# The stand-alone recurrence of a two-layer decoder: order of its work on five engines

## What is computed

```python
def _L0_attn_ref(x, Wk, Wv, Wr, Wo, spatial_decay, spatial_first, mix_k, mix_v, mix_r):
    # q_shift_1d: channels 0..31 come from the token before, 32..63 from the token after, the rest stay
    xx = q_shift_1d(x)
    xk = x * mix_k + xx * (1.0 - mix_k)          # the same for v and r
    k = jnp.einsum('btc,oc->bto', xk, Wk)        # the same for v and r
    sr = jax.nn.sigmoid(r)
    # scan over t with w = decay / T, u = first / T, both states starting at 0:
    #   eku = exp(u + k_t);  out = (a + eku * v_t) / (b + eku);  ek = exp(k_t)
    #   a = a * exp(w) + ek * v_t;  b = b * exp(w) + ek
    return jnp.einsum('btc,oc->bto', sr * wkv_out, Wo)
x = _layernorm(x + _L0_attn_ref(x, ...), axis=-1)
x = _layernorm(x + _L0_xattn_ref(x, ctx_1024, ...), axis=-1)   # and four more sub-layers
```

## Time and profile before

| | |
|---|---|
| median of 3 runs | 2066.99 us (2064.95 to 2070.55) |
| the profiled execution | 2069.05 us, of which 2067.3 us are the span from its first to its last instruction |
| PE busy | 1879.9 us, 91% of the span |
| DVE busy | 1430.0 us, 69% |
| ACT busy | 1191.4 us, 58% |
| POOL busy | 565.3 us, 27% |
| mean granted TensorE clock | 0.961 |
| stage 0 | from the start to 59.65 us, 2.9% of the span |

### The profile page before, as it was taken

How to read it: one execution, slowest core, us unless ns; L and a number is a source line. 1 busy time by engine, 2 the same in 40 slices (tenths; PEclk the granted TensorE clock), 3 DMA queues, 4 the chain that set the end, 5 groups by cost and what they waited for, 6 DMA issues and landing times.

```text
span 2067.3 us, 47928 instructions
## 1 busy us (share of the span) xinstructions
PE 1879.9 (91%) x16935; PEld 1490.1 (72%) x16935; DVE 1430.0 (69%) x3597; ACT 1191.4 (58%) x3980; POOL 565.3 (27%) x894
## 2 busy tenths in 40 slices
PE   3899999999999999999599999788887887699998
PEld 1788888888888888887377777566665554567776
DVE  5578788888887887776465766478786798354443
ACT  1577676676767767766244544277775666133333
POOL 1132222322223221111221221144544576021110
PEclk8899999999999999999799999899999999599999
DMA  7100000000000000000200000100000000000000
GB/s 223 28 2 2 2 2 2 2 2 2 2 2 2 2 2 2 2 2 2 71 1 1 1 1 1 36 2 2 2 2 12 22 12 2 0 0 11 11 4 17
DMA packets 30226, 25.68 MB, mean 12 GB/s; under 512 B 5276, under 2 KB 26788, under 8 KB 29992
## 3 DMA queue, kind: packets, MB, share of 16 engines
q1 hardware_dynamic: 29992, 22.62, 3.8%
HBM read 20.52 MB, written 2.10 MB: 11 GB/s over the span
## 4 chain that ended last, share of the span: by engine, by line
issue 62%; POOL 16%; POOLq 10%; PE 10%; DVE 1%; DMA 0%; DVEq 0%; ACT 0%
POOL X L1817 3%; POOL work L931 3%; PE bank L1938 2%; PE bank L1925 2%; PE bank L1927 2%; POOL work L1608 2%; POOLq L934 2%; POOLq L911 1%; POOL H L935 1%; POOL work L1033 1%; POOL X L1618 1%; PE bank L1905 1%; POOL work L912 1%; POOLq L1607 1%; POOLq L1816 1%
## 5 line engine op out<-in xcount | busy, mean ns | idle before, releaser
L682 ACT ACTIVATE work<-bank,work 128x128 f32<-128x128 f32 x1024 | 363.1, 402 | 208.2 <-DVE work L761 208.2
L523 PE MATMUL bank<-work,wbig 128*128 128x128 f32 x2048 | 262.4, 277 | 0.5 <-ACT work L745 0.5
L523 PEld LDWEIGHTS bank<-work,wbig 128*128 128x128 f32 x2048 | 246.1, 193 | 1.2 <-ACT work L745 0.8
L682 ACT ACTIVATION_READ_ACCUMULATOR work<-bank,work 128x1 f32 x1024 | 246.5, 241 | 0.0
L768 DVE TENSOR_TENSOR work<-work 128x512 f32<-128x512 f32 x256 | 179.1, 700 | 19.8 <-issue 0.9
L761 DVE TENSOR_REDUCE work<-bank 128x4 f32<-128x512 f32 x256 | 159.0, 684 | 33.6 <-PE bank L562 33.6
L697 ACT ACTIVATE work<-bank 128x512 f32<-128x512 f32 x256 | 168.8, 660 | 23.2 <-PE bank L536 23.2
L536 PE MATMUL bank<-ident,work 128*128 128x128 f32 x1024 | 158.1, 277 | 11.8 <-DVE work L768 11.8
L536 PEld LDWEIGHTS bank<-ident,work 128*128 128x128 f32 x1024 | 114.5, 141 | 58.7 <-issue 31.3
L2098 DVE TENSOR_TENSOR work<-wff,bank 128x320 f32<-128x320 f32 (+1 forms) x128 | 62.5, 489 | 127.7 <-ACT wff L2013 127.2
L1167 ACT ACTIVATE work<-bank,col_b 128x512 f32<-128x512 f32 x128 | 87.2, 687 | 106.5 <-PE bank L1095 106.3
(11 more groups left out here) (314 smaller groups left out, 4045.7 us busy)
## 6 DMA issues: line engine op xcount, KB each, us to landing
wbig<-in_moe_w SPq DMA_DIRECT2D x2, 1536.0 KB, 9.2
work<-in_mask_l SPq DMA_DIRECT2D x8, 256.0 KB, 2.9
out<-X SPq DMA_DIRECT2D x8, 256.0 KB, 2.3
H<-in_moe_w SPq DMA_DIRECT2D x3, 512.0 KB, 5.6
wff<-in_moe_w SPq DMA_DIRECT2D x1, 1024.0 KB
X<-in_x SPq DMA_DIRECT2D x1, 512.0 KB, 4.2
wbig<-in_sa_wq SPq DMA_DIRECT2D x1, 512.0 KB, 3.8
wbig<-in_sa_wk SPq DMA_DIRECT2D x1, 512.0 KB, 4.6
```

What stands on the lines that cost most here:

```text
L523: last = nc.tensor.matmul(o[:, j * T:(j + 1) * T], w[:, t * 128:(t + 1) * 128], src, start=True, stop=True)
L682: last = nc.scalar.activation(at_probs[:, g, h, :], bank[g][:, h * T:(h + 1) * T], ACT.Exp, bias=at_nmax[:, g, h:h + 1], accum_out=at_den[ ...
```

## The change

Four things are reordered, and no arithmetic changes.

1. POOL clears the tiles of stage 0 and `b2_sb` first and marks `setup_done`, then clears `keymask` and marks again; the small constants, the tiles of the pairs and `upper` follow without a mark. ACT and VectorE wait for the first mark. VectorE marks, then waits for all four marks before it fills `keymask`. PE waits for all four marks too, but only between the turns and the products.
2. PE turns both groups' tokens first, group 0 into bank 0 and group 1 into bank 7. The output product of group 0 goes to bank 7 and that of group 1 to bank 0.
3. PE forms key and receptance first (mark `rk.kr`), then value (mark `rk.v`). ACT waits for `kr` alone, and VectorE begins with the scan of b, which needs no value, before it waits for `v`.
4. VectorE's `state` is split into `state` and `gate` (reciprocal and z). Its order becomes state(0), gate(0), state(1), residual(0), gate(1), normal(0), residual(1), normal(1). `rk_mv`, `rk_rstd` and `rk_res` get a tile for each group (the second `rk_res` lies on `rk_er[0]`).

The pairs of stage 1 now count on `rk.kr` and `rk.v` instead of semaphores of their own.

```diff
--- before.py
+++ after.py
@@ -129,7 +129,8 @@
 
             xT = sem("rk_xT")
             shift_sb = sem("rk_shift_sb")
-            kvr = sem("rk_kvr")
+            kr = sem("rk_kr")
+            v = sem("rk_v")
             exps = sem("rk_exps")
             gated = sem("rk_gated")
             y = sem("rk_y")
@@ -140,8 +141,6 @@
         class rp:
 
             mixed = sem("rp_mixed")
-            kr = sem("rp_kr")
-            v = sem("rp_v")
             v_sb = sem("rp_v_sb")
             num = sem("rp_num")
             den = sem("rp_den")
@@ -333,37 +332,44 @@
         rk_num = r.take(NB, T)
         rk_den = r.take(NB, T)
         rk_z = [r.take(NB, T) for _ in range(2)]
-        rk_res = r.take(NB, D)
+        rk_res = [r.take(NB, D), rk_er[0]]
         rk_stats = r.take(NB, 6)
-        rk_mv = r.take(NB, 2)
+        rk_mv = [r.take(NB, 2) for _ in range(2)]
         rk_var = r.take(NB)
-        rk_rstd = r.take(NB)
+        rk_rstd = [r.take(NB) for _ in range(2)]
         AHEAD = 2
 
         def flat(ap):
             return ap.rearrange("p b t -> p (b t)")
 
         def rwkv_pe(pe):
+            def turn(g):
+                for b in range(NB):
+                    last = nc.tensor.transpose(bank[7 * g][:, b * T:(b + 1) * T], X[:, NB * g + b, :], ident[:])
+                last.then_inc(rk.xT, 1)
+
+            def product(g, k):
+                o = bank[1 + 3 * g + k]
+                nc.tensor.matmul(o[:], rk_scaled[:, k, 0, :], flat(rk_xT[g]), start=True, stop=False)
+                return nc.tensor.matmul(o[:], rk_scaled[:, k, 1, :], flat(rk_xx[g]), start=False, stop=True)
+
             def front(g):
-                need(pe, rk.shift_sb, g)
-                for b in range(NB):
-                    last = nc.tensor.transpose(bank[0][:, b * T:(b + 1) * T], X[:, NB * g + b, :], ident[:])
-                last.then_inc(rk.xT, 1)
                 pe.wait_ge(rk.shift_sb, g + 1)
-                for k in range(3):
-                    o = bank[1 + 3 * g + k]
-                    nc.tensor.matmul(o[:], rk_scaled[:, k, 0, :], flat(rk_xT[g]), start=True, stop=False)
-                    last = nc.tensor.matmul(o[:], rk_scaled[:, k, 1, :], flat(rk_xx[g]), start=False, stop=True)
-                last.then_inc(rk.kvr, 1)
+                product(g, 0)
+                product(g, 2).then_inc(rk.kr, 1)
+                product(g, 1).then_inc(rk.v, 1)
 
             def back(g):
                 pe.wait_ge(rk.gated, g + 1)
-                need(pe, rk.res_sum, g)
+                pe.wait_ge(rk.shift_sb, 2 - g)
                 for b in range(NB):
-                    last = nc.tensor.matmul(bank[7][:, b * T:(b + 1) * T], rk_z[g][:, b, :], w_rwkv[:, 3, :],
+                    last = nc.tensor.matmul(bank[7 - 7 * g][:, b * T:(b + 1) * T], rk_z[g][:, b, :], w_rwkv[:, 3, :],
                                             start=True, stop=True)
                 last.then_inc(rk.y, 1)
 
+            for g in range(AHEAD):
+                turn(g)
+            pe.wait_ge(setup_done, 4)
             for g in range(AHEAD):
                 front(g)
             for g in range(AHEAD):
@@ -372,25 +378,27 @@
         def rwkv_act(act):
             for g in range(AHEAD):
                 act.wait_ge(rk.xT, g + 1)
-                src = bank[0][:, :].rearrange("p (b t) -> p b t", b=NB)
-                nc.scalar.activation(flat(rk_xT[g]), bank[0][:, :], ACT.Copy)
+                src = bank[7 * g][:, :].rearrange("p (b t) -> p b t", b=NB)
+                nc.scalar.activation(flat(rk_xT[g]), bank[7 * g][:, :], ACT.Copy)
                 nc.scalar.activation(rk_xx[g][0:32, :, 1:T], src[0:32, :, 0:T - 1], ACT.Copy)
                 nc.scalar.activation(rk_xx[g][32:64, :, 0:T - 1], src[32:64, :, 1:T], ACT.Copy)
                 nc.scalar.activation(rk_xx[g][64:128], src[64:128], ACT.Copy).then_inc(rk.shift_sb, 1)
             for g in range(AHEAD):
-                act.wait_ge(rk.kvr, g + 1)
+                act.wait_ge(rk.kr, g + 1)
                 k_ = bank[1 + 3 * g][:, :].rearrange("p (b t) -> p b t", b=NB)
                 nc.scalar.activation(rk_ek[g][:, :, 1:T], k_[:, :, 0:T - 1], ACT.Exp)
                 nc.scalar.activation(flat(rk_eku[g]), bank[1 + 3 * g][:, :], ACT.Exp, bias=rk_u[:, 0:1])
                 nc.scalar.activation(flat(rk_er[g]), bank[3 + 3 * g][:, :], ACT.Exp, scale=-1.0).then_inc(rk.exps, 1)
 
         def rwkv_dve(dve):
+            tt = nc.vector.tensor_tensor
+
             def state(g):
                 dve.wait_ge(rk.exps, g + 1)
+                nc.vector.tensor_tensor_scan(flat(rk_b), flat(rk_ew), flat(rk_ek[g]), 0.0, ALU.mult, ALU.add)
+                dve.wait_ge(rk.v, g + 1)
                 v = bank[2 + 3 * g][:, :].rearrange("p (b t) -> p b t", b=NB)
-                tt = nc.vector.tensor_tensor
                 tt(rk_ekv[:, :, 1:T], rk_ek[g][:, :, 1:T], v[:, :, 0:T - 1], ALU.mult)
-                nc.vector.tensor_tensor_scan(flat(rk_b), flat(rk_ew), flat(rk_ek[g]), 0.0, ALU.mult, ALU.add)
                 tt(flat(rk_num), flat(rk_eku[g]), bank[2 + 3 * g][:, :], ALU.mult)
                 dve.drain()
                 nc.vector.tensor_tensor_scan(flat(rk_a), flat(rk_ew), flat(rk_ekv), 0.0, ALU.mult, ALU.add)
@@ -399,32 +407,37 @@
                 tt(flat(rk_num), flat(rk_num), flat(rk_a), ALU.add)
                 nc.vector.scalar_tensor_tensor(flat(rk_den), flat(rk_er[g]), 1.0, flat(rk_b), ALU.add, ALU.mult)
                 dve.drain()
+
+            def gate(g):
                 nc.vector.reciprocal(flat(rk_den), flat(rk_den))
                 dve.drain()
                 tt(flat(rk_z[g]), flat(rk_num), flat(rk_den), ALU.mult).then_inc(rk.gated, 1)
+                dve.drain()
 
             def residual(g):
                 dve.wait_ge(rk.y, g + 1)
-                nc.vector.tensor_tensor(flat(rk_res), bank[7][:, :], X4[:, g, :], ALU.add).then_inc(rk.res_sum, 1)
+                nc.vector.tensor_tensor(flat(rk_res[g]), bank[7 - 7 * g][:, :], X4[:, g, :], ALU.add).then_inc(rk.res_sum, 1)
                 dve.drain()
                 for b in range(NB):
-                    nc.vector.bn_stats(rk_stats[:, b, :], rk_res[:, b, :])
+                    nc.vector.bn_stats(rk_stats[:, b, :], rk_res[g][:, b, :])
                 dve.drain()
                 for b in range(NB):
-                    last = nc.vector.bn_aggr(rk_mv[:, b, :], rk_stats[:, b, :])
+                    last = nc.vector.bn_aggr(rk_mv[g][:, b, :], rk_stats[:, b, :])
                 last.then_inc(rk.stats, 1)
+                dve.drain()
 
             def normal(g):
                 dve.wait_ge(rk.rstd, g + 1)
                 for b in range(NB):
-                    nc.vector.tensor_scalar(X[:, NB * g + b, :], rk_res[:, b, :], rk_mv[:, b, 0:1], rk_rstd[:, b:b + 1],
-                                            ALU.subtract, ALU.mult)
+                    nc.vector.tensor_scalar(X[:, NB * g + b, :], rk_res[g][:, b, :], rk_mv[g][:, b, 0:1],
+                                            rk_rstd[g][:, b:b + 1], ALU.subtract, ALU.mult)
                 dve.drain()
 
             state(0)
+            gate(0)
+            state(1)
             residual(0)
-            dve.drain()
-            state(1)
+            gate(1)
             normal(0)
             residual(1)
             normal(1)
@@ -432,9 +445,9 @@
         def rwkv_pool(pool):
             for g in range(AHEAD):
                 pool.wait_ge(rk.stats, g + 1)
-                nc.gpsimd.tensor_tensor(rk_var, rk_mv[:, :, 1], lneps[:, 0:NB], ALU.add)
+                nc.gpsimd.tensor_tensor(rk_var, rk_mv[g][:, :, 1], lneps[:, 0:NB], ALU.add)
                 pool.drain()
-                nc.gpsimd.tensor_tensor(rk_rstd, rk_var, half[:, 0:NB], ALU.pow).then_inc(rk.rstd, 1)
+                nc.gpsimd.tensor_tensor(rk_rstd[g], rk_var, half[:, 0:NB], ALU.pow).then_inc(rk.rstd, 1)
                 pool.drain()
 
 
@@ -595,11 +608,11 @@
             def pair_kr(i, o):
                 pe.wait_ge(rp.mixed, 2 * i + 1)
                 pair_product(o, 0, 0)
-                pair_product(o, TWO * T, 2).then_inc(rp.kr, 1)
+                pair_product(o, TWO * T, 2).then_inc(rk.kr, 1)
 
             def pair_v(i, o):
                 pe.wait_ge(rp.mixed, 2 * i + 2)
-                pair_product(o, 0, 1).then_inc(rp.v, 1)
+                pair_product(o, 0, 1).then_inc(rk.v, 1)
 
             def pair_y(i, o):
                 pe.wait_ge(rk.gated, AHEAD + i + 1)
@@ -699,7 +712,7 @@
 
             def pair_shift(i, src):
                 act.wait_ge(rk.xT, AHEAD + i + 1)
-                need(act, rp.v, i)
+                act.wait_ge(rk.v, AHEAD + i)
                 src = src[:, 0:TWO * T].rearrange("p (b t) -> p b t", b=TWO)
                 nc.scalar.activation(rp_xT, src, ACT.Copy)
                 nc.scalar.activation(rp_xx[0:32, :, 1:T], src[0:32, :, 0:T - 1], ACT.Copy)
@@ -707,7 +720,7 @@
```

(25 more changed lines are left out.)

## The result

The changed kernel takes 2056.39 us in the median (2055.06 to 2057.80, 6 runs), the kernel before 2067.89 on the same chips (2064.95 to 2070.56, 6 runs). The ratio is 0.9943, with a 95% interval of 0.9931 to 0.9956: 11.5 us less, as a change of 9 to 14 us. The profiled execution took 2057.20 with a span of 2055.3.

What follows compares the result with a forecast made beforehand. The first stage was taken as bound by a chain from engine to engine; 8.45 us (2.76 from a, 1.25 from b, 4.44 from c) plus 2.11 gave 10.56, so 2066.99 - 10.6 = 2056.4 us, range 2051 to 2062.

Steps and rivals of the forecast that it cites:

- nine links: First stage's chain, from ACT free for the shift (9.72 us) to the next stage's first turn (49.09).
- (c): Key and receptance first: PE's first product to ACT's first exponential takes 6.34 us; 4.44 us of the gain.
- (a): POOL's new clearing order: ACT waits only for the mix columns and is free at 9.72; 2.76 us gained.
- (b): PE turns both groups' tokens before ACT is free: 1.25 us gained; early turns buy no clock.
- (d): VectorE's state(0) starts at 20.13 instead of 28.58, 1.76 us behind the exponentials; value and keymask cost nothing.
- (e): VectorE's interleaving of the groups: the idle 2.17 us before y(0) are covered; z to z shrinks by 2.11 us.
- rival 1: Stage 0's end: engines wait for the last column instead; with landings 3 us later 2058.6 us; chance 0.09.
- Rival 2: Later stage openings: shifted low clock stretches give half back, 5 us over three openings, 2061.4, or reverse, 2052; chance 0.10.

Runs made afterwards that it cites:

- the five undoings: Changed kernel with one part undone each: POOL's order, turns ahead of the wait, group 1's early turns, ACT not waiting for value, interleaving; medians 2061.47, 2059.09, 2060.31, 2059.77, 2059.38.
- The swap: Changed kernel with the two waits at the head of ACT's stream swapped, POOL's mark first, then the mix columns; median 2058.93 us, ratio 0.9954.
- the kernel with the shorter chain: Changed kernel without the reciprocal of group 1, so it doesn't compute the reference; median 2056.69 us, ratio 0.9943.

## Why the prediction was right

**The chain.** The forecast read the first stage as a chain of links and moved each with its duration from the rows. Eight of nine links came out within 0.1 us, and the five undoings started the next stage within 0.2 us of what their links say, but for the 0.7 us of link (c) in the run without POOL's order. The next stage started 11.60 us earlier where 10.56 were summed.

**The term that was mis-sized is (a).** It took ACT's preamble as 2.37 us from its start to its end, table load included, behind the mix columns at 7.25. In the kernel before both waits were over when the load ran, so the earlier trace rows couldn't show which of them the load stood behind. In the changed kernel it needs POOL's mark alone, and 1.28 of the 2.37 us are hidden in the wait for the columns: 8.59 instead of 9.72, with the columns in at 7.40 rather than 7.25. That it was hidden is luck: nothing in the forecast asked in which order the two waits are written. The swap puts them back (+1.33). The sign I gave for being wrong in (a) was a table load *later* than 7.3; it came earlier. The first exponential at 17.30 lies just outside the 17.4 to 19.1 that I gave for (c), for this reason only: link (c) itself was 6.31 for 6.34.

**(b), (c).** Right: the turns were hidden, and the clock rose where group 0's did before. In the eleven kernels in which ACT waited for key and receptance alone (the changed kernel and all experiments but the two that made it wait for more), first product to first exponential took between 5.58 and 6.65 us, inside the bounds of -1.0 and +0.7. The rise is read from the products, 0.86 and then 0.43 us apart; the profile's granted clock reads 1.00 over both, and only from the later low stretch of the earlier trace rows (0.51) is it seen that 0.86 apart goes with the lower level. That early turns buy no clock isn't shown: with identical code up to the first exponential the link took 5.93 to 6.62, and the two extremes of position, turns over 7.2 us ahead of the products (5.58, without POOL's order) and 1.5 us ahead (6.11, turns behind the wait), differ by less than that.

**(d), (e).** Right, link by link; value was never waited for, keymask's 4.97 us ended at 14.2, and y(0) was covered.

**The loads (rival 1).** The margin was read rightly as thin, but the cap was put in the wrong place. The forecast set the column's landing, 48.3, against PE's first turn and capped the gain at 11.3 us; the gain at that turn was 11.60, and it came at 48.05. PE's turn doesn't wait for rows and columns, ACT's copy 0.6 us behind it does. That copy had 1.1 us in hand over the last column in the profiled execution, and would have had 0.2 with the latest landing seen; the kernel with the shorter chain ran into it, and got 0.1 of 3.8 us. The changed kernel is within about a microsecond of what this list of waits allows.

**The median.** That 2056.39 meets 2056.4 is partly luck. I subtracted 10.6 from 2066.99; with three more runs the kernel before stands at 2067.89, and the gain was 11.5. The excess is, within the runs' spread, the mis-sized term's 1.1. Rival 2 (the clock elsewhere) exists, with about 2.7 us beside one added low stretch, more than the 1.65 that I gave one, and fell on neither side in the medians.

## What to carry to other kernels

Where no engine is busy for long, read the stage as a chain: ask of each link what its start waits for, and look for work that stands in an engine's order ahead of what the chain needs (here group 1's turns and shift, value's product, a residual that waits for PE); moving it is worth its full length. Then find what is late next before shortening further: a wait on a group of loads is as late as its last member, even one that the stage never reads, and in the kernel with the shortened chain splitting that group freed 3.0 us, where reordering the loads freed 0.6.

## What the hardware showed that I hadn't expected

- The activation table load (1.28 us) ran ahead of a wait that is written in front of it: in the changed kernel it started at 3.88, on POOL's mark, though the wait for the mix columns (7.40) is written first. In the other orders it stood behind the last-written wait, the mix columns at 7.44 when the two were swapped and PE's turns at 6.85 when ACT's first activation was a shift. That only the last-written one ever counts fits all of these, but only the first order tests it. Why is not shown by these runs.
- Moving the 2 MB context load behind seventeen smaller ones didn't free the list: it was issued at 32.58 and landed at 47.2, where the last column of the changed kernel landed at 47.5.
- One extra low stretch of TensorE's clock (1600 to 1610 us) goes with about 2.7 us more, far from any edit. It is as large as one of the links measured here, which is why the start of the next stage and not the median had to carry the verdicts.
